# Hyperedge loop of a graph kernel: a fresh PSUM sum for every round, added on GpSimd, with the operand splits four tiles ahead

## The chip, the cores and the metric

The program runs on one core of a Trainium2 chip. The metric is the device time of one execution in microseconds (us). The core's engines run side by side and each takes its own instructions in order: TensorE (PE, with the loading of weights shown as PEld), VectorE (DVE), ScalarE (ACT), GpSimd (POOL), and SyncE for DMA. Semaphores order the work between engines.

## The reference, cut to what matters

Eight graphs (B) share 1024 nodes (N) and 64 hyperedges (E); features are 64 wide (F). The kernel computes four layers one after another, each with a residual and a layer norm. The change is in the first, in its hyperedge attention:

```
beta   = sigmoid((h @ a_gn)[:, None, :] + (agg @ a_ge)[:, :, None])
all_he = elu(beta * h + (1 - beta) * agg)            # for every (hyperedge, node) pair
coefs1 = softmax(where(H > 0, se, NEG), axis=-1)     # over the hyperedges of a node
g      = einsum('bne,benf->bnf', coefs1, all_he)
```

H is sparse (a node has about three hyperedges), so the kernel works only on the pairs that exist. What it sums for a node is the numerator (512 columns: 8 graphs times 64 features) and the denominator Z of the softmax (8 columns); g is their quotient.

## The kernel before

Nodes are on the 128 partitions, in NT = 8 tiles. The existing (node, hyperedge) pairs of a tile are listed one after another and taken in rounds of CHUNKS = 3 chunks (A, B, C) of 128 pairs. How many rounds a tile needs is known only on the chip (`first[t]` to `first[t + 1]`), so each engine runs, for each tile t, a loop `Fori(first[t], first[t + 1]) as j`. With this input every tile takes one round (line 908, which runs three times in a round, runs 24 times), so there are eight turns of the loop.

What one round does, by engine and line:

- DVE `from_first` and `to_last` (L742, L745) build NSF, the one-hot matrix that says which node each pair belongs to. They do it for the next round. `edges` (L749) builds EST, the same for hyperedges, from the sums that PE made (`edge_rows`, L655).
- PE `turn_edges` (L665) and `turn_nodes` (L660) transpose EST and NSF into PSUM bank 6. ACT copies them out as SELF and SELG (L828) and as NST (L866); `nodes_copy` (L831) makes NSG, a copy of NSF.
- PE `small_sums` (L671, L672) fetches the logits' parts, `gather` (L677 to L680) fetches h (as a high part HPH and a low part HPL) and agg for the pairs of a chunk. Chunk C is gathered in its own round, chunks B and A in the round before.
- DVE `mix` (L778), `shift` (L783), ACT `grow` (L862), DVE `bend` (L787) make the elu of a chunk; GpSimd multiplies it with the softmax weights CC (L908, and L903 for CC itself).
- PE `scatter` (L711) multiplies the result with NST and adds it to PSUM bank 4; the three matmuls of L733 add the weights to bank 7.

PSUM sums of a tile run over all its rounds. They are set to zero by a product of zeros at the head of each tile (L703, L704, bf16), and at the end of the tile ACT copies them out to GN and ZS (L886, L887). PE waits for that copy (`acc_out`) before it sets the banks to zero again. The order within each engine is written out by hand.

The high part HPH of h is made by ACT (L825) and the low part HPL by GpSimd (`low`, L895), each two tiles ahead: tiles 0 and 1 before the loop, tile t + 2 at the end of tile t. Also at the end of tile t, DVE takes the reciprocal of Z of tile t - 1 (L814) and GpSimd scales GN of tile t - 1 by it (L914); tile 7 is scaled by DVE after the loop (L816, L818). The block then ends, and the next block of the kernel begins on PE at L1026.

## Time and profile before

| | |
|---|---|
| median of 3 runs | 904.74 us (903.09, 904.74, 904.85) |
| the profiled execution | 903.21 us in all, its span 901.4 us |
| TensorE | 740.9 us busy, 82% of the span |
| VectorE | 439.6 us, 49% |
| ScalarE | 336.2 us, 37% |
| GpSimd | 293.2 us, 33% |
| mean granted clock of TensorE | 0.906 of full speed |
| the loop of this change on PE | from 152.4 us (first L703) to 241.7 us (end of the last L733) |

The span runs from the first to the last instruction; the device time of the same execution is 1.8 us longer. Busy times overlap, so they don't add up to the span. In the rows below, times are microseconds from the start of the span; "x3" is a count of instructions that the view has merged; a bracket behind a row tells how long the engine had been idle and which instruction (or "issue": nothing that the profile shows) ended that. A mean of one instruction is in nanoseconds.

### The profile page before, as it was taken

The numbers are of one execution on the slowest core, as the hardware profiler recorded it, in microseconds if no ns is written. First come the engines' busy times: TensorE is split into PE (matmuls) and PEld (weight loads), VectorE is DVE, ScalarE is ACT, GpSimd is POOL, SyncE is SP. The second block draws the span as 40 slices with busy tenths as digits, with TensorE's granted clock in tenths as the row PEclk, the third lists the DMA queues.
The fourth block names the chain that finished last, engine by engine and source line by source line (L and its number), as shares of the span: only waits on it lengthen the run. The fifth ranks groups of instructions, "written<-read, shape, count | busy, mean of one in ns | idle before, by whom it ended". The sixth has DMA issues, their size and how long they took to land. (4 is left out here: it accounts for less than half of the span.)

```text
span 901.4 us, 10005 instructions
## 1 busy us (share of the span) xinstructions
PE 740.9 (82%) x3518; PEld 506.5 (56%) x3518; DVE 439.6 (49%) x982; ACT 336.2 (37%) x628; POOL 293.2 (33%) x265
## 2 busy tenths in 40 slices
PE   3956985898897549899898983997888888899990
PEld 3646874666664448533232322786666666678880
DVE  1484353777448741245464666311355464562165
ACT  1741212445464121256353542222233536363110
POOL 0430001445365420000003149001356565651055
PEclk9967995999999669999998996899999899999995
DMA  8200002000000000000000000000000000000013
GB/s 278 80 14 1 1 1 93 1 1 1 1 1 1 0 1 1 1 0 1 1 0 1 0 12 38 1 1 1 0 1 1 1 1 0 1 1 1 1 24 70
DMA packets 12949, 14.36 MB, mean 16 GB/s; under 512 B 9680, under 2 KB 9680, under 8 KB 12896
## 3 DMA queue, kind: packets, MB, share of 16 engines
q1 hardware_dynamic: 11408, 11.61, 4.0%
q10 hardware_dynamic: 1488, 2.06, 0.8%
q8 instruction: 32, 0.52, 0.2%
q14 instruction: 21, 0.17, 0.1%
HBM read 11.57 MB, written 2.10 MB: 15 GB/s over the span
## 5 line engine op out<-in xcount | busy, mean ns | idle before, releaser
L1619 DVE SCALAR_TENSOR_TENSOR arena<-PS,WT,arena 128x256 f32<-128x256 f32 x160 | 77.4, 484 | 88.0 <-PE PS L1736 64.3
L1329 DVE TENSOR_REDUCE arena<-PS 128x1 f32<-128x1024 f32 x64 | 75.5, 1220 | 76.3 <-PE PS L1165 76.3
L1252 ACT ACTIVATE arena<-PS,arena 128x1024 f32<-128x1024 f32 x64 | 70.8, 1110 | 72.4 <-DVE arena L1329 72.4
L1165 PE MATMUL PS<-arena 64*128 64x512 f32 x256 | 77.4, 626 | 4.8 <-ACT arena L1252 2.5
L163 POOL TENSOR_TENSOR LN_Y<-LN_V,CN 128x16 f32<-128x16 f32 (+1 forms) x17 | 50.2, 2951 | 87.6 <-DVE LN_V L155 87.6
L1723 PE MATMUL PS<-WH,KH 128*128 128x512 f32 x128 | 55.4, 432 | 25.4 <-ACT XX L1537 20.7
L1549 ACT ACTIVATE SY<-PS,WT 128x256 f32<-128x256 f32 x96 | 38.5, 471 | 100.2 <-DVE arena L1619 100.2
L1272 POOL TENSOR_TENSOR arena<-arena 128x128 f32<-128x128 f32 x32 | 12.9, 403 | 188.0 <-DVE arena L1333 188.0
L1183 PE MATMUL PS<-arena 128*64 128x512 f32 x256 | 63.6, 620 | 1.2 <-POOL arena L1272 1.1
L1165 PEld LDWEIGHTS PS<-arena 64*128 64x128 f32 x256 | 28.5, 187 | 51.4 <-issue 32.0
L1723 PE MATMUL PS<-WH,KL 128*128 128x512 f32 x128 | 52.2, 408 | 0.0
L1723 PE MATMUL PS<-WL,KH 128*128 128x512 f32 x128 | 51.9, 405 | 0.0
L1723 PEld LDWEIGHTS PS<-WH,KH 128*128 128x128 f32 x128 | 24.9, 195 | 38.6 <-ACT XX L1537 23.8
L1183 PEld LDWEIGHTS PS<-arena 128*64 128x64 f32 x256 | 16.2, 140 | 46.5 <-issue 44.1
L1461 POOL TENSOR_TENSOR KL<-XX,KH 128x1024 fp32r<-128x1024 f32 x8 | 19.0, 2379 | 64.9 <-ACT KH L1539 64.9
L908 POOL TENSOR_TENSOR arena<-arena,CC 128x512 f32<-128x512 f32 x24 | 25.0, 1043 | 43.3 <-DVE arena L787 43.3
L895 POOL TENSOR_TENSOR HPL<-arena,HPH 128x512 fp32r<-128x512 f32 x8 | 10.2, 1277 | 81.0 <-ACT HPH L825 81.0
L140 DVE BATCH_NORM_STATS2 LN_ST<-arena 128x6 f32<-128x64 f32 x256 | 35.3, 211 | 2.1 <-POOL arena L1480 1.6
L283 POOL TENSOR_TENSOR ADJL<-arena,ADJH 128x1024 fp32r<-128x1024 f32 x8 | 19.7, 2486 | 43.4 <-ACT ADJH L295 43.4
L1765 PE MATMUL PS<-ADJH,NH 128*128 128x512 f32 x128 | 33.4, 394 | 0.5 <-ACT NH L1560 0.5
L1774 PE MATMUL PS<-ADJH,NL 128*128 128x512 f32 x128 | 32.8, 390 | 0.0
L1041 PE MATMUL PS<-arena,WT 128*128 128x512 f32 x64 | 32.0, 647 | 0.0
(265 smaller groups left out, 1631.4 us busy)
## 6 DMA issues: line engine op xcount, KB each, us to landing
arena<-in_adj_tr SPq DMA_DIRECT2D x8, 512.0 KB, 8.3
arena<-in_x_tr SPq DMA_DIRECT2D x4, 512.0 KB, 9.3
arena<-in_x_nat SPq DMA_DIRECT2D x1, 2048.0 KB, 8.4
...
```

The source lines that it names most:

```text
L140: ins = dve.bn_stats(LN_ST[:, i, :], source(i))
L163: pool.tensor_tensor(LN_Y[:, at:at + n], LN_V[:, at:at + n], CN[:, C_NEGH:C_NEGH + n], ALU.pow).then_inc(ln_rstd, 1)
L1041: pe.matmul(PS[:, 4 + v % HRING, :], wt(W_FC + (b % 2) * P, P), FT[:, (2 if w else 0) + q % 2, half * HALF:(half + 1) * HALF], start=True, ...
L1165: ins = pe.matmul(banks("S", 2 * i + par)[:, half, :], KT[q % 2][r, tile(m)], QT[q % 2][r, c], start=True, stop=True)
L1183: ins = pe.matmul(PS[r, 6 + half, :], AVN[:, i % RING, par, :], EF[2 * (i % RING) + par][:, c], start=(m == 0), stop=(m == NT - 1), skip_g ...
L1252: act.activation(EF[2 * (i % RING) + par], banks("S", 2 * i + par).rearrange("p a c -> p (a c)"), ACT.Exp, bias=NMX[:, i, par:par + 1], ac ...
L1329: dve.tensor_reduce(NMX[:, i, par:par + 1], banks("S", 2 * i + par), AX.XY, ALU.max, negate=True).then_inc(max_ready, 1)
L1549: act.activation(groups(SY[:, n % SYS, :]), PS[:, four_banks(t, j), d * F:(d + 1) * F], ACT.Copy, scale=WT[:, e:e + 1]).then_inc(sy_ready, 1)
L1619: dve.scalar_tensor_tensor(acc, PS[:, four_banks(t, j), d * F:(d + 1) * F], WT[:, e:e + 1], acc, ALU.mult, ALU.add).then_inc(acc_step, 1)
L1723: ins = pe.matmul(acc, x[:, t % 2, b, :], w[:, k, c], start=(first and n == 0), stop=(not first and n == 2), skip_group_check=True)
L1765: pe.matmul(acc[:, half, :], NH[:, m, tile(q)], ADJH[:, m, c], start=(m == 0), stop=False, skip_group_check=True)
L1774: ins = pe.matmul(acc[:, half, :], NL[:, m, tile(q)], ADJH[:, m, c], start=False, stop=(m == NT - 1), skip_group_check=True)
```

## The change

- **Sums.** The products of zeros and `zero16` are gone. The first `scatter` of every round starts bank 4 afresh (`start=(c == A_)`), and likewise the first of the three L733 matmuls bank 7. After every round ACT copies bank 4 to ROUND_SUM (in XX, a tensor that a later stage uses too and that is now allocated earlier) and the Z columns to ROUND_Z, and GpSimd adds them to ZS and GN, which it has set to zero once before the loop. `acc_raw` says that ACT has copied, `acc_out` that GpSimd has added.
- **Order on PE.** The waits for `acc_out` at the head of a tile go; `scatter(A_)` waits for `acc_raw`. `scatter(A_)` goes behind `small_sums`, `scatter(B_)` behind `gather(A_)` and `turn_nodes`. `turn_nodes` reads NSG in place of NSF.
- **Order on DVE.** `from_first` and `to_last` go to the head of the round, ahead of the mixes; `bend` of A goes behind `edges`, `bend` of C behind `logits`.
- **Order on ACT.** The copy of NST goes from the head of a round to its end, before the copies of the sums.
- **Ahead.** The high and low parts are made four tiles ahead: tiles 0 to 3 before the loop, tile t + 4 at the end of tile t. On GpSimd `low` now stands behind L914's scaling.

```diff
@@ -233,7 +233,6 @@
         DG = arena[:, 0:B * E].rearrange("p (b e) -> p b e", e=E)
         SEB = arena[:, B * E:2 * B * E].rearrange("p (b e) -> p b e", e=E)
         LGM = arena[:, 2 * B * E:4 * B * E].rearrange("p (a b e) -> p a b e", a=2, e=E)
-        zero16 = sb("zero16", [P, 512], BF16)
         ONR = sb("ONR", [P, 2], F32R)
         rest_max = sb("rest_max", [P, NT + 1])
         has_rest = sb("has_rest", [1, 1], I32)
@@ -274,7 +273,6 @@
                 pool.memset(SM[:, :], 0.0).then_inc(sl, 1)
                 pool.memset(AGBD[:, :, :], 0.0).then_inc(zero_set, 1)
                 pool.memset(HM[:, :, :], 0.0).then_inc(zero_set, 1)
-                pool.memset(zero16[:, :], 0.0).then_inc(zero_set, 1)
                 pool.wait_ge(sl, 1)
                 pool.memset(SM[0:64, 16:17], 1.0).then_inc(zero_set, 1)
                 for t in range(NT):
@@ -455,7 +453,7 @@
                 link(dve.tensor_tensor(AGM[:, :, :], AGM[:, :, :],
                                        wt(W_GE, F).unsqueeze(1).broadcast_to([P, BP, F]), ALU.mult))
                 link(dve.tensor_reduce(ae[:, :], AGM[:, :, :], AX.X, ALU.add))
-                dve.wait_ge(zero_set, 4)
+                dve.wait_ge(zero_set, 3)
                 for par in range(2):
                     r = slice(64 * par, 64 * par + 64)
                     dve.tensor_scalar(SM[r, par:B:2], ae[r, :], 0.5, None, ALU.mult)
@@ -613,8 +611,9 @@
         CC = sb("CC", [P, CHUNKS, B])
         ZS = sb("ZS", [P, NT, B])
         iota = CN[:, C_IOTA:C_IOTA + ROUND].rearrange("p (c n) -> p c n", n=P)
-        SMALL_AT, ZN_AT = CHUNKS * E, 0
+        SMALL_AT = CHUNKS * E
         A_, B_, C_ = range(CHUNKS)
+        AHEAD = 4
         bank_of = (0, 1, 0)
 
         fold_ready, agh_ready, agl_ready, agn_ready, hph_ready, hpl_ready = (
@@ -625,7 +624,10 @@
         ts_ready, lg_ready, thh_ready, xc_ready, be_ready, cc_ready, gath_ready, m_ready, z_ready, e_ready, t_ready, w_ready = (
             sem(s) for s in ("ts_ready", "lg_ready", "thh_ready", "xc_ready", "be_ready", "cc_ready", "gath_ready", "m_ready",
                              "z_ready", "e_ready", "t_ready", "w_ready"))
-        acc_done, acc_out, rn_ready, g_done = (sem(s) for s in ("acc_done", "acc_out", "rn_ready", "g_done"))
+        acc_done, acc_raw, acc_out, rn_ready, g_done = (sem(s) for s in ("acc_done", "acc_raw", "acc_out", "rn_ready", "g_done"))
+        XX = sb("XX", [P, B, 2, F])
+        ROUND_SUM = XX[:, 0:B // 2, :, :].rearrange("p b k f -> p (b k f)")
+        ROUND_Z = sb("ROUND_Z", [P, B])
 
         def first_rounds(eng):
             return [eng.value_load(first_i[0:1, t:t + 1], min_val=0, max_val=NT * ROUNDS) for t in range(NT + 1)]
@@ -657,7 +659,7 @@
 
                 def turn_nodes():
                     for c in range(CHUNKS):
-                        ins = pe.transpose(PS[:, 6, tile(c)], NSF[:, c, :], ident)
+                        ins = pe.transpose(PS[:, 6, tile(c)], bits(NSG[:, c, :]), ident)
                     ins.then_inc(nt_ready, 1)
 
                 def turn_edges():
@@ -698,17 +700,15 @@
                 pe.wait_ge(agl_ready, 1)
                 pe.nop().then_inc(acc_done, 1)
                 for t in range(NT):
-                    if t >= 1:
-                        pe.wait_ge(acc_out, t)
-                    pe.matmul(PS[:, 4, :], zero16[:, 0:P], zero16[:, :], start=True, stop=False, skip_group_check=True)
-                    pe.matmul(PS[:, 7, ZN_AT:ZN_AT + B], zero16[:, 0:P], zero16[:, 0:B], start=True, stop=False, skip_group_check=True)
                     pe.wait_ge(hpl_ready, min(t + 2, NT))
                     with pe.Fori(first[t], first[t + 1]) as j:
                         k_next, t_next = next_round(j, t, first)
 
                         def scatter(c):
                             pe.wait_ge(w_ready, CHUNKS * j + (c + 1))
-                            return pe.matmul(PS[:, 4, :], NST[:, c, :], S1[:, c, :], start=False, stop=True, skip_group_check=True)
+                            if c == A_:
+                                pe.wait_ge(acc_raw, j + 1)
+                            return pe.matmul(PS[:, 4, :], NST[:, c, :], S1[:, c, :], start=(c == A_), stop=(c == C_), skip_group_check=True)
 
                         pe.wait_ge(ns_ready, j + 2)
                         edge_rows(t_next)
@@ -717,20 +717,20 @@
                         pe.wait_ge(nst_out, j + 1)
                         pe.wait_ge(est_ready, j + 2)
                         turn_edges()
-                        scatter(A_)
                         pe.wait_ge(self_ready, j + 2)
                         small_sums(t_next)
+                        scatter(A_)
                         pe.wait_ge(nsg_ready, j + 2)
                         pe.wait_ge(selg_ready, j + 2)
                         pe.wait_ge(z_ready, CHUNKS * j + 2)
                         gather(t_next, B_)
-                        scatter(B_)
                         pe.wait_ge(z_ready, CHUNKS * j + 3)
                         gather(t_next, A_)
                         turn_nodes()
+                        scatter(B_)
                         scatter(C_)
                         for c in range(CHUNKS):
-                            ins = pe.matmul(PS[:, 7, ZN_AT:ZN_AT + B], NST[:, c, :], CC[:, c, :], start=False, stop=True,
+                            ins = pe.matmul(PS[:, 7, 0:B], NST[:, c, :], CC[:, c, :], start=(c == A_), stop=(c == C_),
                                             skip_group_check=True)
                         ins.then_inc(acc_done, 1)
 
@@ -786,33 +786,32 @@
                             dve.wait_ge(e_ready, CHUNKS * j + (c + 1))
                             dve.scalar_tensor_tensor(S1[:, c, :], S1[:, c, :], 1.0, S0[:, c, :], ALU.min, ALU.max).then_inc(t_ready, 1)
 
+                        dve.wait_ge(nsg_ready, j + 1)
+                        from_first(at).then_inc(ns_half, 1)
+                        dve.wait_ge(ns_half, j + 2)
+                        to_last(at).then_inc(ns_ready, 1)
                         dve.wait_ge(be_ready, j + 1)
                         mix(B_, 1)
                         mix(A_, 2)
-                        dve.wait_ge(selg_ready, j + 1)
-                        dve.wait_ge(nt_ready, j + 1)
-                        from_first(at).then_inc(ns_half, 1)
                         shift(A_, 2)
-                        dve.wait_ge(ns_half, j + 2)
-                        to_last(at).then_inc(ns_ready, 1)
                         shift(B_, 1)
-                        bend(A_)
                         dve.wait_ge(r_ready, j + 2)
                         dve.wait_ge(sT_ready, j + 1)
                         edges(k_next)
+                        bend(A_)
                         mix(C_, 3)
                         bend(B_)
                         shift(C_, 3)
                         dve.wait_ge(small_ready, j + 2)
                         dve.wait_ge(cc_ready, j + 1)
                         small_out()
-                        bend(C_)
                         dve.wait_ge(ts_ready, j + 2)
                         logits()
+                        bend(C_)
                     if t >= 1:
-                        dve.wait_ge(acc_out, t)
+                        dve.wait_ge(acc_out, first[t] + 1)
                         dve.reciprocal(ZS[:, t - 1, :], ZS[:, t - 1, :]).then_inc(rn_ready, 1)
-                dve.wait_ge(acc_out, NT)
+                dve.wait_ge(acc_out, first[NT] + 1)
                 dve.reciprocal(ZS[:, NT - 1, :], ZS[:, NT - 1, :]).then_inc(rn_ready, 1)
                 dve.wait_ge(rn_ready, NT)
                 dve.tensor_tensor(groups(GN[:, NT - 1, :]), groups(GN[:, NT - 1, :]), spread(ZS[:, NT - 1, :]), ALU.mult)
@@ -839,6 +838,7 @@
                 def likely():
                     act.activation(XC[:, :, :], LG[:, :, :], ACT.Exp).then_inc(xc_ready, 1)
 
+                act.nop().then_inc(acc_raw, 1)
                 act.wait_ge(fold_ready, 1)
                 act.activation(AGS[:, :], PS[:, 7, :], ACT.Copy).then_inc(agh_ready, 1)
                 high(0)
@@ -855,15 +855,16 @@
                 sigmoid()
                 act.wait_ge(lg_ready, 1)
                 likely()
+                act.wait_ge(nt_ready, 1)
+                edges_out(NST, nst_out)
+                for t in range(2, AHEAD):
+                    high(t)
                 for t in range(NT):
                     with act.Fori(first[t], first[t + 1]) as j:
                         def grow(c):
                             act.wait_ge(z_ready, CHUNKS * j + (c + 1))
                             act.activation(S1[:, c, :], S0[:, c, :], ACT.Exp, bias=CN[:, C_M1:C_M1 + 1]).then_inc(e_ready, 1)
 
-                        act.wait_ge(nt_ready, j + 1)
-                        act.wait_ge(acc_done, j + 1)
-                        act.activation(NST[:, :, :], PS[:, 6, 0:ROUND].rearrange("p (c n) -> p c n", n=P), ACT.Copy).then_inc(nst_out, 1)
                         grow(A_)
                         grow(B_)
                         act.wait_ge(sT_ready, j + 2)
@@ -880,11 +881,14 @@
                         act.wait_ge(lg_ready, j + 2)
                         act.wait_ge(cc_ready, j + 1)
                         likely()
-                    if t + 2 < NT:
-                        high(t + 2)
-                    act.wait_ge(acc_done, first[t + 1] + 1)
-                    act.activation(GN[:, t, :], PS[:, 4, :], ACT.Copy)
-                    act.activation(ZS[:, t, :], PS[:, 7, ZN_AT:ZN_AT + B], ACT.Copy).then_inc(acc_out, 1)
+                        act.wait_ge(nt_ready, j + 2)
+                        act.wait_ge(acc_done, j + 2)
+                        edges_out(NST, nst_out)
+                        act.wait_ge(acc_out, j + 1)
+                        act.activation(ROUND_SUM, PS[:, 4, :], ACT.Copy)
+                        act.activation(ROUND_Z[:, :], PS[:, 7, 0:B], ACT.Copy).then_inc(acc_raw, 1)
+                    if t + AHEAD < NT:
+                        high(t + AHEAD)
 
             @block.gpsimd
             def _(pool):
@@ -894,8 +898,11 @@
                     pool.wait_ge(hph_ready, t + 1)
                     pool.tensor_tensor(HPL[:, t, :], HP[:, t, :], bits(HPH[:, t, :]), ALU.subtract).then_inc(hpl_ready, 1)
 
-                low(0)
-                low(1)
+                for t in range(AHEAD):
+                    low(t)
+                pool.memset(ZS[:, :, :], 0.0)
+                pool.memset(GN[:, :, :], 0.0).then_inc(acc_out, 1)
+                pool.wait_ge(acc_out, 1)
                 for t in range(NT):
                     with pool.Fori(first[t], first[t + 1]) as j:
                         pool.wait_ge(xc_ready, j + 1)
@@ -907,12 +914,16 @@
                             pool.wait_ge(t_ready, CHUNKS * j + (c + 1))
                             pool.tensor_tensor(groups(S1[:, c, :]), groups(S1[:, c, :]), spread(CC[:, c, :]),
                                                ALU.mult).then_inc(w_ready, 1)
-                    if t + 2 < NT:
-                        low(t + 2)
+                        pool.wait_ge(acc_raw, j + 2)
+                        pool.wait_ge(acc_out, j + 1)
+                        pool.tensor_tensor(ZS[:, t, :], ZS[:, t, :], ROUND_Z[:, :], ALU.add)
+                        pool.tensor_tensor(GN[:, t, :], GN[:, t, :], ROUND_SUM, ALU.add).then_inc(acc_out, 1)
                     if t >= 1:
                         pool.wait_ge(rn_ready, t)
                         pool.tensor_tensor(groups(GN[:, t - 1, :]), groups(GN[:, t - 1, :]), spread(ZS[:, t - 1, :]),
                                            ALU.mult).then_inc(g_done, 1)
+                    if t + AHEAD < NT:
+                        low(t + AHEAD)
 
 
         FT = feature_major(0)
@@ -1356,7 +1367,6 @@
         X2 = node_major(3)
         XA = node_major(4)
         X3 = node_major(3)
-        XX = sb("XX", [P, B, 2, F])
         ZH = rounded("ZH", 5 * SLOT, [P, NT, BF])
         ZL = rounded("ZL", 6 * SLOT, [P, NT, BF])
         AH = rounded("AH", 0, [P, NT, BF])
```

## Rows read from the trace of the kernel before

**Rows 1.** Two turns: length; busy PE, PEld, DVE, ACT, POOL (instructions); TensorE clock, DMA.

```profile
177.90:188.60 10.70, 9.46 (x51) 6.71 (x51) 8.21 (x18) 5.49 (x14) 5.60 (x6) 1.00 0.01 2
188.60:200.50 11.90, 10.88 (x50) 7.57 (x51) 8.18 (x18) 5.50 (x14) 5.60 (x6) 0.86 0.00 0
```

**Rows 2.** Timeline from the end of one round's sums to the next: start, length, engine, line.

```profile
175.77 0.73 PE L733 MATMUL PS<-CC,arena 128*128 128x8 f32 x6
...
176.54 0.60 ACT L886 ACTIVATE arena<-PS 128x512 f32<-128x512 f32 x1 [2.85 <-PE PS L733]
...
177.26 0.10 PEld L703 LDWEIGHTS PS<-zero 128*128 128x128 bf16 x1 [0.84 <-ACT ZS L887]
...
177.46 1.39 ACT L862 ACTIVATE arena<-arena,CN 128x512 f32<-128x512 f32 x2
...
177.92 0.88 PE L655 MATMUL PS<-arena 128*128 x6 [0.26 <-issue]
...
178.97 0.87 DVE L749 TENSOR_SCALAR arena<-PS,CN 128x128 f32<-128x128 f32 x3
...
179.98 0.52 PE L665 MATMUL PS<-CN,arena 128*128 128x128 f32 x3 [0.20 <-DVE arena L749]
...
180.34 1.02 PE L711 MATMUL PS<-arena 128*128 128x512 f32 x2
...
180.42 0.68 DVE L787 SCALAR_TENSOR_TENSOR arena<-arena 128x512 f32<-128x512 f32 x1
180.54 0.49 ACT L828 ACTIVATE SELF<-PS 128x384 fp32r<-128x384 f32 x1 [1.69 <-PE PS L665]
...
181.20 0.29 PE L671 MATMUL PS<-SM,SELF 128*128 128x17 f32 x2
...
182.46 0.48 PE L677 MATMUL PS<-HPH,NSG 128*128 x1
...
184.53 1.28 POOL L895 TENSOR_TENSOR HPL<-arena,HPH 128x512 fp32r<-128x512 f32 x1
...
185.77 1.04 POOL L914 TENSOR_TENSOR arena<-arena,ZS 128x512 f32<-128x512 f32 x1
...
186.44 0.73 PE L733 MATMUL PS<-CC,arena 128*128 128x8 f32 x6
```

**Rows 3.** The page's costliest groups: GpSimd's multiplication by the weights.

```profile
L908 POOL TENSOR_TENSOR arena<-arena,CC 128x512 f32<-128x512 f32 x24 | 25.0, 1043 | 43.3 <-DVE arena L787 43.3
```

**Rows 4.** Groups of GpSimd's instructions by shape: count, busy us, mean ns, idle before.

```profile
L1480 POOL TENSOR_TENSOR arena<-arena,AGBD 128x512 f32<-128x512 f32 x4 | 5.2, 1292 | 0.6
L903 POOL TENSOR_TENSOR CC<-XC,TS 128x24 f32<-128x24 f32 x8 | 2.0, 246 | 6.8 <-PE PS L733 5.7 <-ACT XC L840 1.1
...
L275 POOL MEMSET AGBD<- 128x512 f32 x1 | 0.5, 524 | 0.0
L276 POOL MEMSET HM<- 128x136 f32 x1 | 0.2, 211 | 0.0
```

**Rows 5.** Timelines of DVE and GpSimd in the stage behind the loop.

```profile
265.37 1.23 DVE L952 TENSOR_TENSOR arena<-arena,KP 128x1024 f32<-128x1024 f32 x1
265.45 3.35 POOL L984 TENSOR_TENSOR arena<-arena 128x1024 f32<-128x1024 f32 x1
266.63 3.26 DVE L955 TENSOR_TENSOR arena<-arena 128x1024 f32<-128x1024 f32 x1
```

**Rows 6.** Timeline of the first round: turned nodes, first scatter, last sums.

```profile
152.70 0.49 ACT L866 ACTIVATE arena<-PS 128x384 f32<-128x384 f32 x1 [3.14 <-PE PS L660]
...
158.85 1.14 PE L711 MATMUL PS<-arena 128*128 128x512 f32 x2
...
165.06 0.73 PE L733 MATMUL PS<-CC,arena 128*128 128x8 f32 x6
```

**Rows 7.** Timeline of the loop's end and of the next block's first PE work.

```profile
240.96 0.73 PE L733 MATMUL PS<-CC,arena 128*128 128x8 f32 x6
...
242.66 0.69 DVE L818 TENSOR_TENSOR arena<-arena,ZS 128x512 f32<-128x512 f32 x1
...
243.66 1.24 PE L1026 MATMUL PS<-CN,arena 128*128 128x128 f32 x8 [1.98 <-PEq L642]
```

## The prediction, as it was put on record

> **What bounds the kernel now.** I read the page's head first (TensorE 82% busy, GpSimd 33%), then the busy time by stretch, then the timeline of one turn of the loop, since only there does an average turn into an order. In a turn PE is busy for 9.46 of 10.70 us; the next turn lasts 11.90 with nothing different in it but a granted clock of 0.86, that is, a piece of it at the lower of the two levels, 1.2 GHz [rows 1]. So PE bounds the loop, with one hole. The timeline shows the hole [rows 2]: the sums end at 176.50 (175.77 + 0.73; I call this moment Z), ACT copies bank 4 and Z out, PE is released at 177.26, sets the banks to zero, and begins the next round's products at 177.92, 1.42 after Z. From Z to Z (187.17) the turn takes 10.67. The page's groups show what GpSimd does meanwhile: its 24 multiplications of 1.04 us have 43.3 us of idle time before them, all ended by DVE [rows 3]. It is an engine with time to spare, and its end-of-tile work (`low` at 184.53, the scaling at 185.77, done at 186.81) lies ahead of Z, where nobody waits for it [rows 2]. That last point decides my forecast.
>
> **What the change takes away.** The two products of zeros and PE's wait for ACT: PE can begin `edge_rows` right behind Z, because `to_last` now stands at the head of DVE's round. The most this can give: from Z, edge_rows 0.88, edges 0.87, turn_edges 0.52, the SELF copy 0.49 [rows 2], with signals 3.0 us. (ACT gives the same: 1.15 for its copies, below, and 1.39 for two `grow`.) Then small_sums, 1.26 (181.20 to 182.46), then scatter A and the rest of the turn. The rest is 6.83 before (180.34 to 187.17), with the small sums in it, so 5.57 without them. 3.0 + 1.26 + 5.57 = 9.85, 0.8 less than 10.67. What had hidden the SELF copy was scatter A; it now stands behind small_sums, and this price is in the 3.0.
>
> **What it puts in the way.** Scatter A needs GpSimd's product w A. Before w A, GpSimd must now, in program order, wait for ACT's copy of the round's sums, add them, scale the tile before (L914), make `low(t + 4)`, and make CC. All of it was done before Z or didn't exist; now all of it begins after Z. Step by step, from Z:
> - ACT: NST copy, then the two copies. Before, the two took until 0.76 (177.26). With a copy of about 0.5 ahead, of which some 0.1 overlaps the next, `acc_raw` comes at 1.15.
> - GpSimd: the ZS add, 8 columns, isn't in the trace; CC with 24 columns takes 0.25 [rows 4], so 0.2. The GN add is two plain operands of 512 columns, as L1480, 1.29 [rows 4] (from below, the 1.04 of L914, whose second operand is a broadcast [rows 2]). Done at 2.65.
> - L914 1.04, `low` 1.24 by the distance to the next start (184.53 to 185.77) [rows 2], CC 0.2, w A 1.04 [rows 3] and a signal: 6.2.
> - PE's remaining 5.57: Z again at 11.8.
>
> So that is for tiles 2 to 4 (turns in which both L914 and `low` stand ahead). Turn 1 has no L914: 10.8. Turns 5 to 7 have no `low`: 10.55. This is by GpSimd's order alone.
>
> **The price of sharing.** GpSimd's work behind Z reads SBUF while DVE runs `bend` (L787, 0.68 [rows 2]), whose two inputs are both in SBUF. Before, bend and GpSimd hardly overlap. Elsewhere in this trace they do [rows 5]: L984 on GpSimd starts 0.08 after DVE's L952 and lasts 3.35; DVE's L955 starts at 266.63, and though it's of L952's shape (1.23) it takes 3.26, ending 1.09 after L984 (268.80). Each waited until the other was through; only about 0.14 of its time overlapped. So bend A, ready near 2.0, waits for the GN add, runs 0.54 past it, and L914 waits for bend A; bend B then goes between L914 and `low` in the same way. Each handover costs GpSimd 0.54 less 0.10 to 0.14, about 0.44; two make 0.9. Turns: 12.7 (three), 11.7 (turn 1), 11.45 (three). I take this case; the bound from below is no price at all.
>
> The Trainium skill has this as a rule: SBUF — State Buffer, section "Who interferes with whom", says that a DVE instruction with two SBUF inputs and a GpSimd instruction that reads SBUF take an exclusive lock, the later one blocking fully. By that rule the trace agrees, with the 3.26 against 1.23; the rule speaks against this change, and without it the sum below is 5.6 instead of 12.4.
> Of GpSimd's records the skill says (Perfetto Trace Analysis, section "Per-engine timelines") that one should go by the distance from start to start and not by the reported span. By that the multiplications would count a few hundredths less each, and the sum some 0.1 less a turn.
>
> **The sum.** Turns 1 to 7 took 241.69 - 165.79 = 75.9 [rows 6, 7]. After: 11.7 + 3 x 12.7 + 3 x 11.45 = 84.15, so +8.2. The 75.9 holds the slow-clock piece of one turn, 1.2 [rows 1]; whether it comes again is even, so +0.6.
>
> First turn: the turned nodes are out at 152.66 (L866 begins at 152.70). Then NST, `high(2)`, `high(3)` on ACT; `low(2)` can begin near 153.8, both end near 156.3. Then GN is set to zero: 4096 columns. 136 columns take 0.21 and 512 take 0.52 [rows 4], 0.83 ns each, so 3.5 (eight times 0.52, 4.2, from above; it can't be hidden since `acc_out` is waited for right behind). CC and w A end at 161.3. Scatter A starts then and not at 158.85 [rows 6], but the small sums are done by that time, and 5.57 later it is 166.9 against 165.79: +1.1.
>
> End: before, Z to the last multiplication's end was 1.66 (241.69 to 243.35), and the next block's PE began 0.3 later [rows 7]. After, acc_raw 1.15, adds to 2.65, reciprocal and multiplication: 3.6. But GpSimd scales tile 6 just then (2.65 to 3.7), with L818 also reading two SBUF inputs, so 4.2. +2.0 to +2.5; I take 2.5.
>
> 8.2 + 0.6 + 1.1 + 2.5 = +12.4. Removed besides: one zero16 fill at the start, under the input's loading, and nothing else; priced at nothing. Turning NSG in place of NSF costs the same, as the shape is the same. On the profiled execution (903.21, its span 901.4 and 1.8 around it) this gives 915.6; the median of the runs is 1.5 higher, 904.74, and gives 917.1. I say 917.
>
> **The rivals.**
> - *Only the queue, no lock* (the bends escape the overlap): turns 10.8, 3 x 11.8, 3 x 10.55 = 77.85, +1.95; with 0.6, 1.1 and 2.0 this is +5.6: 910.3. For it: bend A may slip in before the GN add starts. Against: rows 5. Chance 0.20.
> - *The hole closes and GpSimd keeps up*: PE's own 9.85 decides, seven turns give 7 x (10.84 - 9.85) = 6.9 against the mean turn of before, less 3.1 for first turn and end, about -3.5: 901. It needs w A by 4.3 after Z; the break-even is a turn of 10.4, w A by 4.8. GpSimd's shortest tail (no `low`) is 1.15 + 0.2 + 1.29 + 1.04 + 0.2 + 1.04 = 4.9, so its true times would have to be well under the records. For it: its spans are rough. Against: its back-to-back starts (184.53, 185.77) agree with them. Chance 0.06.
> - *No change*: the same with w A near 4.8: 904.7. Chance 0.04.
> - *The clock falls too*: PE now stands still for 2 to 3 us in every turn, ahead of scatter A. For it: the hole before, 1.42 us, went with one such fall in two turns shown [rows 1, 2], and PE's hole grows. Against: the other turn had the same hole and none. A turn's piece at the low level costs 1.2 [rows 1]; in four to seven turns, +5 to +8: 922 to 925. Chance 0.10.
> - The forecast, queue and lock: 0.60, its own range 914 to 920.
>
> **How the numbers follow.** About 0.2% (1.8 us) is what a measurement of this kernel can tell from no change. Slower by more: 0.60 + 0.20 + 0.10 = 0.90. Within: 0.04. Faster: 0.06. The range takes in the first two cases and the edge of the clock's: 908.5 to 921.
>
> **What the profile after would show.** Right: the first L711 of a round starts 6 to 7.3 us after Z, behind a wait for GpSimd's multiplication; GpSimd's GN add starts 1.2 to 1.4 after Z, and its L914, `low`, CC follow without a wait for another engine; turns of tiles 2 to 4 are 1.2 longer than those of 5 to 7; `bend` of A and B last over 1 us where a GpSimd record lies beside them. PE starts `edge_rows` within 0.2 of Z. Wrong: `bend` stays at 0.68 (the lock), L711 waits for nothing (the queue), PE's clock falls in most turns, or the zero fill takes far from 3.5 us.

## The result, and the profile after

The changed kernel takes 931.62 us (median of 4 runs, 928.07 to 933.20), the kernel before 903.91 on the same chip (902.92 to 904.85): a ratio of 1.0301 [1.0266, 1.0337]. It is slower, as forecast, but by 27.7 us where I had said 12.4, and outside the range.

The profiled execution took 930.43 us, its span 928.6; TensorE's mean granted clock is 0.896 (before 0.906). First the page's groups that wait for each other: the end of a row is the idle time ahead of the group and what ended it.

```profile
L711 PE MATMUL PS<-arena 128*128 128x512 f32 x48 | 29.9, 737 | 17.3 <-POOL arena L915 17.3
L899 POOL TENSOR_TENSOR HPL<-arena,HPH 128x512 fp32r<-128x512 f32 x8 | 12.4, 1560 | 86.3 <-ACT HPH L824 86.3
```

PE now waits 17.3 us for GpSimd ahead of its scatters (L711): 4.59 in the first round, 2.25 to 2.40 in turns 2 to 4, about 1.4 in the other four; before, it had no such wait. The busy time by stretch, cut at the moments Z (the ends of the rounds' L733 sums), answers to [rows 1]: length; busy PE, PEld, DVE, ACT, POOL; TensorE clock, DMA.

```profile
169.66:183.10 13.44, 10.93 (x49) 7.51 (x50) 10.04 (x17) 5.12 (x13) 7.01 (x7) 0.87 0.00 0
183.10:198.86 15.76, 12.26 (x51) 8.57 (x50) 10.38 (x17) 5.23 (x13) 8.35 (x8) 0.78 0.00 1
198.86:213.61 14.75, 11.41 (x49) 7.93 (x50) 10.39 (x17) 5.23 (x13) 8.35 (x8) 0.77 0.00 1
213.61:227.87 14.26, 10.77 (x51) 7.44 (x50) 10.39 (x17) 5.24 (x13) 8.35 (x8) 0.88 0.01 2
227.87:241.09 13.22, 10.95 (x51) 7.53 (x50) 10.32 (x17) 4.72 (x12) 6.78 (x7) 0.87 0.00 0
...
190.50:196.50 6.00, 6.00 (x14) 4.10 (x15) 3.94 (x6) 0.00 (x0) 2.34 (x2) 0.50 0.00 0
```

Two things are to be read there. PE is not only idle longer, its busy time grew too, from 9.46 [rows 1] to 10.8 to 12.3, for the same matmuls (less the two products of zeros). And no turn has the clock 1.00; the last row is a piece of the second turn at 0.50, the 1.2 GHz level, with PE busy all through. The timeline of that turn shows how it comes about (start, length, engine, line), for [rows 2]:

```profile
183.20 0.49 ACT L827 ACTIVATE arena<-PS 128x384 f32<-128x384 f32 x1 [6.82 <-PE PS L733]
...
184.33 0.21 POOL L919 TENSOR_TENSOR ZS<-ZS,ROUND_Z 128x8 f32<-128x8 f32 x1 [5.64 <-ACT ROUND_Z L889]
...
184.49 1.27 POOL L920 TENSOR_TENSOR arena<-arena,XX 128x512 f32<-128x512 f32 x1
...
185.41 0.90 DVE L787 SCALAR_TENSOR_TENSOR arena<-arena 128x512 f32<-128x512 f32 x1 [0.55 <-ACT arena L866]
185.72 1.49 POOL L923 TENSOR_TENSOR arena<-arena,ZS 128x512 f32<-128x512 f32 x1
...
186.42 0.40 PE L673 MATMUL PS<-SM,SELF 128*128 128x17 f32 x2 [0.90 <-ACT SELF L827]
...
187.18 1.71 POOL L899 TENSOR_TENSOR HPL<-arena,HPH 128x512 fp32r<-128x512 f32 x1
...
188.85 0.23 POOL L910 TENSOR_TENSOR CC<-XC,TS 128x24 f32<-128x24 f32 x1
...
189.24 3.60 POOL L915 TENSOR_TENSOR arena<-arena,CC 128x512 f32<-128x512 f32 x3 [0.17 <-POOL CC L910]
...
189.52 1.31 DVE L787 SCALAR_TENSOR_TENSOR arena<-arena 128x512 f32<-128x512 f32 x1
...
190.33 2.08 PE L711 MATMUL PS<-arena 128*128 128x512 f32 x2 [2.40 <-POOL arena L915]
...
198.13 0.73 PE L733 MATMUL PS<-CC,arena 128*128 128x8 f32 x6
```

From Z (183.10) GpSimd works without a pause: the ZS add, the GN add, the scaling (L923), `low` (L899), CC, w A (L915). Scatter A (L711) starts at 190.33, 7.23 after Z, and then takes 2.08 for what took 1.02 [rows 2]: PE had stood still for 2.40, and in that wait, at about 189.7, the granted clock went to the lower level, until about 196.6. In the other turns too it falls once, from 0.5 us before such a wait begins to 1.1 us after it has ended. The rest of the turn, from scatter A to the next Z, takes 8.53 and not 5.57. `bend` (L787) lasts 0.90, 0.93 and 1.31 for A, B and C beside GpSimd's records, 0.68 when alone [rows 2]. PE has a second hole that the kernel before had not, ahead of its small sums (L673), where it waits for the SELF copy: 0.90 in turns 1 to 4, 0.66 in turns 5 to 7.

All seven turns, each as (Z to scatter A) + (rest): 6.24 + 7.20, 7.23 + 8.53, 7.23 + 7.52, 7.23 + 7.03, 6.00 + 7.22, 6.00 + 7.18, 5.99 + 7.16; in all 97.76 against 75.90. GpSimd ahead of the first round, for [rows 6], and the loop's end, for [rows 7]:

```profile
153.70 3.04 POOL L899 TENSOR_TENSOR HPL<-arena,HPH 128x512 fp32r<-128x512 f32 x2 [5.25 <-ACT HPH L824]
156.69 0.15 POOL L903 MEMSET ZS<- 128x64 f32 x1
156.77 3.52 POOL L904 MEMSET arena<- 128x4096 f32 x1
160.94 0.23 POOL L910 TENSOR_TENSOR CC<-XC,TS 128x24 f32<-128x24 f32 x1 [0.66 <-POOL arena L904]
161.35 2.49 POOL L915 TENSOR_TENSOR arena<-arena,CC 128x512 f32<-128x512 f32 x2 [0.18 <-POOL CC L910]
...
268.65 0.20 POOL L919 TENSOR_TENSOR ZS<-ZS,ROUND_Z 128x8 f32<-128x8 f32 x1 [5.77 <-ACT ROUND_Z L889]
268.81 1.26 POOL L920 TENSOR_TENSOR arena<-arena,XX 128x512 f32<-128x512 f32 x1
270.03 1.04 POOL L923 TENSOR_TENSOR arena<-arena,ZS 128x512 f32<-128x512 f32 x1
...
270.34 1.28 DVE L817 TENSOR_TENSOR arena<-arena,ZS 128x512 f32<-128x512 f32 x1
271.93 1.30 PE L1037 MATMUL PS<-CN,arena 128*128 128x128 f32 x5 [4.50 <-PEq L644]
```

Scatter A of the first round starts at 162.44, Z comes at 169.66 (before 165.79): +3.9. The next block's PE begins 4.51 after the last Z (267.42), before 1.97: +2.5. So 21.9 + 3.9 + 2.5 = 28.3; the rest of the program is 1.1 shorter, and the spans differ by 27.2.

### The profile page after: what moved, and what is told of

It reads as the page before. It is cut to its first block and busy times, and to the rows that moved or that the text cites. A ratio compares the mean times of both kernels' runs of the same rounds, so it can differ in the third digit from the quotient of the medians.

```text
span 928.6 us, 9999 instructions
## 1 busy us (share of the span) xinstructions
PE 751.0 (81%) x3502; PEld 513.1 (55%) x3502; DVE 458.9 (49%) x982; ACT 334.6 (36%) x629; POOL 316.7 (34%) x282
## 5 line engine op out<-in xcount | busy, mean ns | idle before, releaser
L1283 POOL TENSOR_TENSOR arena<-arena 128x128 f32<-128x128 f32 x32 | 12.9, 403 | 186.9 <-DVE arena L1344 186.9
L711 PE MATMUL PS<-arena 128*128 128x512 f32 x48 | 29.9, 737 | 17.3 <-POOL arena L915 17.3
L899 POOL TENSOR_TENSOR HPL<-arena,HPH 128x512 fp32r<-128x512 f32 x8 | 12.4, 1560 | 86.3 <-ACT HPH L824 86.3
L1484 POOL TENSOR_TENSOR YP<-YP,SY 128x256 f32<-128x256 f32 x32 | 23.8, 743 | 22.3 <-ACT SY L1559 18.9
```

## The experiments

Times are medians beside runs of the kernel before on the same chip, whose medians are 902.74 us for 1 to 4, 900.84 for 5 to 8, 902.87 for 9 to 12 and 904.34 for 13 to 16. A ratio is to that kernel; it is taken over the runs and differs a little from the quotient of the medians. The turns are those of one profiled execution each. The part of the program behind the loop, which no edit touches, takes 655.7 to 662.6 us in these profiles, so a few us between two medians are no measure of the turns. "Products of zeros" compute nothing: they write a bank that is overwritten later.

**1. The fill of GN and ZS ahead of the first low parts.**

```diff
-                for t in range(AHEAD):
-                    low(t)
                 pool.memset(ZS[:, :, :], 0.0)
                 pool.memset(GN[:, :, :], 0.0).then_inc(acc_out, 1)
+                for t in range(AHEAD):
+                    low(t)
```

> The changed kernel with one edit: GpSimd sets GN and ZS to zero before it makes the first low parts, in time in which it had nothing to do, and not behind them. My theory: in the first round the 3.5 us fill stands between the low parts and the first product that PE waits for, so scatter A starts 4.2 us earlier (at about 158.2 us and not 162.4), PE hardly stands still, its clock stays up and the rest of the round takes 5.6 and not 7.2 us: 5 to 6 us less in all, near 926. All later turns as they were. Rival (the fill lies beside other work, and the first round waits for its small sums or its copies): less than 1 us.

926.69 us, 1.0259 [1.0222, 1.0296]: 23.9 us above the kernel before, not 27.7. Scatter A of the first round starts at 158.47, not 162.44, so the start that the first round lost was the fill's place. The other half of the theory missed: the clock falls in this round too (157.4 to 164.2), its rest takes 8.31 and not 5.6, and Z comes only 2.9 earlier. That 926 was met all the same is luck. The waits of the turns are as before this edit (6.24, three of 7.23, three of 6.00 to scatter A), their rests 1.5 longer in all.

**2. Scaling and `low` inside the round, ahead of its wait for the sums** (the same work where each tile has one round, as with these inputs).

```diff
+                        if t >= 1:
+                            pool.wait_ge(rn_ready, t)
+                            pool.tensor_tensor(groups(GN[:, t - 1, :]), groups(GN[:, t - 1, :]), spread(ZS[:, t - 1, :]),
+                                               ALU.mult).then_inc(g_done, 1)
+                        if t + AHEAD < NT:
+                            low(t + AHEAD)
                         pool.wait_ge(acc_raw, j + 2)
```

> The changed kernel with GpSimd's scaling of the tile before and its low part moved ahead of its wait for the round's sums (inside the round, which is the same where a tile has one round, as with this input). Theory, queue on GpSimd plus the clock: behind the end of the sums only the addition, CC and the first product are left, the product is there 4.3 us after it, when PE has just done its small sums, PE waits for nothing, its clock stays up: turns of 9.9 to 10.4 us in place of 13.2 to 15.8, in all 24 to 28 us less, 904 to 908, no worse than the kernel before by more than 4. Rival A, the new order on PE is what costs (the copy of the transposed edges lies open): turns stay above 12. Rival B, the clock falls for a reason other than PE's wait: the wait goes, turns of 11.5 us, about 916.

926.82 us, 1.0279 [1.0243, 1.0315]: the theory missed. Turns 1 to 4 stay above 12, as rival A had it, but for a reason that none of the three named. The timeline of turn 1, from Z = 168.02:

```profile
168.12 0.49 ACT L827 ACTIVATE arena<-PS 128x384 f32<-128x384 f32 x1 [7.93 <-PE PS L733]
...
169.04 0.64 ACT L824 ACTIVATE HPH<-arena 128x512 fp32r<-128x512 f32 x1
...
169.76 1.27 POOL L899 TENSOR_TENSOR HPL<-arena,HPH 128x512 fp32r<-128x512 f32 x1 [6.73 <-ACT HPH L824]
...
174.77 2.07 PE L711 MATMUL PS<-arena 128*128 128x512 f32 x2 [1.92 <-POOL arena L915]
```

`low(t + 4)` needs ACT's `high(t + 4)`, which ACT makes behind its copies of the sums. So `low` can't come ahead of Z here, and the adds now stand behind it. Turns 5 to 7 have no `low` and are free of it. Turns 5 and 6 show the second thing:

```profile
223.28:233.43 10.15, 9.29 (x49) 6.57 (x48) 8.40 (x14) 4.72 (x12) 6.32 (x7) 1.00 0.00 0
233.43:248.96 15.53, 13.87 (x51) 9.97 (x50) 10.97 (x21) 4.95 (x12) 6.25 (x7) 0.67 0.01 1
```

Both have no wait for GpSimd. The first is the turn the change could have had, 10.15; the second has the same work at clock 0.67 and takes 15.53 (turn 7: 11.66 at 0.85).

**3. Products of zeros in PE's wait**, the same kernel otherwise: nothing is taken from GpSimd, only PE's standing still.

```diff
                         small_sums(t_next)
+                        for _ in range(20 if t == 0 else 12 if 2 <= t <= 4 else 7):
+                            pe.matmul(PS[:, 7, 64:64 + 440], zero16[:, 0:P], zero16[:, 0:440], start=True, stop=True)
                         scatter(A_)
```

> The changed kernel with products of zeros (bf16, 440 columns, into columns of bank 7 that nobody reads) put on PE between its small sums and scatter A: 20 in the first round, 12 in rounds 2 to 4, 7 in the others, which fill most of its wait for GpSimd. They compute nothing. Theory, PE's standing still lets its clock fall: scatter A starts as late as before (7.2 and 6.0 us after the end of the sums), but the rest of the turn takes 5.6 in place of 7.0 to 8.5 us, in all 10 to 14 us less, 918 to 922. Rival, the clock falls for another reason (or the end of a turn is long for its new order of instructions): no change, 930 to 933.

922.26 us, 1.0199 [1.0168, 1.0229]; the profiled execution is the slowest of six, 930.22. Turns 1 and 6:

```profile
169.57:181.40 11.83, 10.63 (x58) 7.19 (x57) 9.71 (x17) 5.13 (x13) 7.01 (x7) 1.00 0.01 1
238.14:249.74 11.60, 10.63 (x58) 7.19 (x57) 10.00 (x17) 4.72 (x12) 6.79 (x7) 1.00 0.00 0
```

Scatter A starts 6.24 and 6.01 after Z, as without the fills, and the rest is 5.59 in both: these are the turns of my forecast (11.7 and 11.45), to 0.15. In turns 2 to 5 and 7 the clock still fell, in part ahead of the fills (in turn 2 at 185.9, the fills begin at 186.24); they then ran at the lower level, twelve in 3.89, and past the wait (scatter A at 8.57, 9.56, 8.30, 6.40, 7.00). In turns 4 and 5 it fell with the fills already running, when only the hole ahead of the small sums was left. So turns 1 and 6 show what the rest of a turn costs when the clock stays up, and speak for PE's standing still in the wait as the cause; five turns of seven don't decide it, and as a cure these fills are a poor one. More on the cause comes from 13 and 16.

**4. `low` ahead of the wait as in 2, and in its old place a fill (1,400 columns) of the same length**, which reads nothing. It changes no result, as tiles ahead are set to zero again.

```diff
+                        if t + AHEAD < NT:
+                            low(t + AHEAD)
                         pool.wait_ge(acc_raw, j + 2)
                         ...
                     if t + AHEAD < NT:
-                        low(t + AHEAD)
+                        pool.memset(GN[:, t + 1:t + 4, :].rearrange("p t c -> p (t c)")[:, 0:1400], 0.0)
```

> The changed kernel with the low part made ahead of GpSimd's wait, and in its old place a fill with zeros of 1400 columns (about the same 1.26 us, of tiles of GN that are still zero), which reads nothing. The queue on GpSimd is as long as it was; only the sharing between bend of chunk B and the low part is gone. Theory, lock: bend of B takes no longer than bend alone beside the fill, the fill starts right behind the scaling, and scatter A of turns 1 to 4 starts 0.4 to 0.5 us earlier (5.8 and 6.8 in place of 6.24 and 7.23 us after the end of the sums), 1.5 to 2 us in all. Rival, no lock, GpSimd just takes this long: 7.2 stays.

939.06 us, 1.0410 [1.0368, 1.0451]. Missed, for the reason found in 2: `low` waits for ACT, so both it and the fill are behind Z (scatter A at 7.50, then 8.95 three times). It says nothing of the lock; 7 and 8 ask that again.

**5. The change's orders alone:** the sums as before (banks set to zero, ACT copies them once a tile, no adds on GpSimd), all orders of PE, DVE and ACT as changed.

```diff
+                    if t >= 1:
+                        pe.wait_ge(acc_out, t)
+                    pe.matmul(PS[:, 4, :], zero16[:, 0:P], zero16[:, :], start=True, stop=False, skip_group_check=True)
                     ...
-                        pool.tensor_tensor(ZS[:, t, :], ZS[:, t, :], ROUND_Z[:, :], ALU.add)
-                        pool.tensor_tensor(GN[:, t, :], GN[:, t, :], ROUND_SUM, ALU.add).then_inc(acc_out, 1)
```

> The changed kernel's orders on PE, DVE and ACT, its splits four tiles ahead and the turned NSG, but the sums as before (a tile's sums stay in PSUM, products of zeros, ACT copies them straight to GN and ZS; no addition on GpSimd). Theory: the orders alone cost little; PE is released 1.2 us after the end of the sums, the chain of edge rows, edges, turned edges and their copy ends at 4.5, small sums and the rest of 5.6: turns of 11.4 against 10.7, about 5 us more than the kernel before, near 908. Rival A, the orders are the main loss of the change: over 918. Rival B, they are a gain on their own: under 902.

925.44 us, 1.0278 [1.0206, 1.0350]. My own theory missed: rival A holds. Without the adds and with no wait for GpSimd in the turns, the loss is nearly the same. Turns 1 and 3:

```profile
165.23:181.25 16.02, 13.96 (x50) 9.95 (x50) 9.84 (x18) 5.35 (x13) 5.71 (x6) 0.68 0.00 0
194.76:206.70 11.94, 9.69 (x51) 6.77 (x50) 8.42 (x16) 5.24 (x13) 5.71 (x6) 1.00 0.00 1
```

A turn at full clock takes 11.94 (6.38 + 5.56); three of the seven took about 16 with the clock low for two thirds of them.

**6. All low parts, and ACT's high parts, ahead of the loop** (with 1), so that no `low` stands behind Z.

```diff
-        AHEAD = 4
+        AHEAD = NT
```

> The changed kernel with all eight high and low parts made before the loop (ACT's and GpSimd's idle time there) and GN set to zero before them; nothing but the scaling stays behind the addition. Theory: turn 1 (no scaling) needs no wait on PE, 9.9 to 10.4 us; turns 2 to 7 are as turns 5 to 7 of the changed kernel, scatter A 6.0 us after the end of the sums, 13.2 us each; first round over at about 163.5 instead of 169.7: 912 to 920. Rival (the low parts' cost is hidden): no more than e1, 926.

920.67 us, 1.0202 [1.0160, 1.0244], just above what was expected. Turn 1 takes 4.56 + 5.59 = 10.15; turns 2 to 7 take 6.00 + (7.16 to 8.05). Here too the queue is as forecast (5.9), and the clock takes 1.6 to 2.5 on top.

**7 and 8. The lock by itself.** As 6, with one more GpSimd operation in the tail of tiles 1 to 3, where `low` stood: in 7 the subtraction that `low` is, into a spare buffer; in 8 a fill of the same length, which reads nothing.

```diff
+                    if t < 4:
+                        pool.tensor_tensor(SPARE, bits(HPL[:, t, :]), bits(HPH[:, t, :]), ALU.subtract)
```

```diff
+                    if t < 4:
+                        pool.memset(GN[:, t + 1:t + 4, :].rearrange("p t c -> p (t c)")[:, 0:1400], 0.0)
```

> As e7_all_ahead, with a subtraction of the low part's shape (its result is not used) put on GpSimd behind the scaling, at the end of tiles 0 to 3, where the changed kernel makes its low parts. It reads SBUF as they do, but waits for nothing. Theory: turn 1 has scatter A 6.2 and turns 2 to 4 have it 7.2 us after the end of the sums, as in the changed kernel; 919 to 926.

> As e9_read_in_tail, with a fill with zeros of 1400 columns (1.26 us) in place of the subtraction: as long, but reads nothing. Theory, lock: bend of chunk B doesn't wait beside it, and it doesn't wait for bend; scatter A comes 0.4 to 0.5 us earlier than in e9 in turns 1 to 4 (5.8 and 6.8 us after the end of the sums), 1.5 to 2.5 us in all. Rival, no lock and only the length of GpSimd's work: as e9 within 0.1 us a turn.

928.38 us, 1.0290 [1.0242, 1.0338] and 924.25 us, 1.0257 [1.0218, 1.0297]. GpSimd's records of one tail, of 7 and then of 8:

```profile
183.59 1.71 POOL L929 TENSOR_TENSOR XX<-HPL,HPH 128x512 f32<-128x512 f32 x1
185.27 0.22 POOL L913 TENSOR_TENSOR CC<-XC,TS 128x24 f32<-128x24 f32 x1
```

```profile
180.62 1.26 POOL L928 MEMSET arena<- 128x1400 f32 x1
181.85 0.23 POOL L912 TENSOR_TENSOR CC<-XC,TS 128x24 f32<-128x24 f32 x1
```

Scatter A of turns 2 to 4 starts at 7.23, 7.23, 7.24 in 7 and at 6.76 three times in 8. The operation that reads takes 1.71 with a `bend` between, the one that only writes 1.26: 0.46 to 0.48 a turn, where I had priced a handover at 0.44. The waits of the turns make 1.9 of the 4.1 us between the two medians, as expected; the rest of the 4.1 isn't theirs. Experiment 7 lies 2.4 above its range.

**9. The add one round late**, so that GpSimd adds the sums of round j - 1 while PE works on j, with all of 6.

```diff
-                        pool.wait_ge(acc_raw, j + 2)
+                        pool.wait_ge(acc_raw, j + 1)
                         pool.wait_ge(acc_out, j + 1)
-                        pool.tensor_tensor(GN[:, t, :], GN[:, t, :], ROUND_SUM, ALU.add).then_inc(acc_out, 1)
+                        pool.tensor_tensor(g_sum, g_sum, ROUND_SUM.unsqueeze(1), ALU.add).then_inc(acc_out, 1)
```

> As e7_all_ahead, with the addition of a round's sums one round later: GpSimd adds the sums of round j - 1 behind the three products of round j, and those of the last round behind the loop. Behind the end of the sums only CC and the products are left. Theory, GpSimd's queue: no turn waits for it, each is like turn 1 of e7, 10.15 us where the clock stays up, the first round as in e7; with no fall of the clock about 897, 5 less than the kernel before; the hole of 0.7 to 0.9 us ahead of the small sums is left in every turn, so some falls of 1.6 to 5 us each must be expected: 896 to 906. Rival, the clock falls in most turns all the same: 908 to 915.

926.94 us, 1.0269 [1.0232, 1.0306]. Missed. There is no wait for GpSimd's w A any more and turns of 10.01 to 10.68 appear, but every second one takes 16.2 to 16.8, with the clock at 0.50 for 10.2 us:

```profile
179.20:189.40 10.20, 8.86 (x26) 6.54 (x26) 5.72 (x12) 3.90 (x9) 4.29 (x5) 0.50 0.01 2
```

Behind it stand new holes that I hadn't seen: DVE's reciprocal now waits for the late add, ahead of `from_first`, and PE's `edge_rows` comes 1.35 late.

**10. Experiment 9 with three products of zeros ahead of the small sums.** The edit is that of 13 below, with three.

> As e8_all_ahead_lag, with three products of zeros (bf16, 440 columns, into bank 1 before it is gathered into) on PE between the turned edges and the small sums, where PE waits for the copy of the turned edges. They compute nothing. Theory, PE's standing still is what lets the clock fall: the turns of e8 at the lower clock become turns at the full one, 10.15 to 10.4 us each, 895 to 900. Rival, the hole has nothing to do with it: as e8.

920.47 us, 1.0226 [1.0165, 1.0286]; turns 10.68, 13.23, 12.85, 16.42, 10.01, 17.13, 10.03: with this one hole filled the others still bring falls.

**11 and 12. The orders taken apart.** In 11 PE's order is that of before and the others (DVE's, ACT's, GpSimd's) are changed; 12 is the kernel before with PE's order alone:

```diff
                         turn_edges()
-                        scatter(A_)
                         pe.wait_ge(self_ready, j + 2)
                         small_sums(t_next)
+                        scatter(A_)
                         ...
                         gather(t_next, B_)
-                        scatter(B_)
                         pe.wait_ge(z_ready, CHUNKS * j + 3)
                         gather(t_next, A_)
+                        scatter(B_)
```

> As e5_orders_only, but with PE's order of before (scatter A ahead of the small sums, scatter B ahead of gather A): what is left of the change are DVE's and ACT's orders, the turned NSG and the splits four tiles ahead. Theory, after e5 (925.4): what e5 lost came from PE standing still twice in a turn, for ACT's copies (now 0.4 later) and for the copy of the turned edges; without the second, turns of about 11.1 us at full clock and falls in few of them: 904 to 912. Rival, the 0.4 us on ACT are enough for the clock: over 918.

> The kernel before with nothing but PE's order of after: scatter A behind the small sums, scatter B behind gather A and the turned nodes. Theory, after e5: the copy of the turned edges (0.5 us) lies open, small sums start 4.6 us after the end of the sums, scatter A 5.85, turns of 11.4 us at full clock, and the two holes together bring the clock down in several of the seven turns: 908 to 920. Rival A, the order alone is harmless: 901 to 906. Rival B, it is the whole loss of e5: 922 or more.

11: 929.43 us, 1.0297 [1.0262, 1.0331], missed; PE waits 1.11 for w A in the five turns at full clock, since DVE makes `edges` ahead of `bend` A and w A waits for that `bend` (its record starts 1.16 late for it); two turns take 16.0 and 16.1. 12: 918.08 us, 1.0200 [1.0139, 1.0261]. Its turns 1 to 3, and PE's holes in turn 2:

```profile
164.24:179.89 15.65, 13.88 (x49) 9.77 (x50) 7.97 (x18) 5.38 (x13) 5.59 (x6) 0.67 0.00 0
179.89:191.31 11.42, 9.47 (x50) 6.77 (x50) 7.93 (x17) 5.41 (x13) 5.60 (x6) 1.00 0.01 2
191.31:204.32 13.01, 11.05 (x49) 7.77 (x50) 8.14 (x19) 5.40 (x13) 5.59 (x6) 0.87 0.00 0
```

```profile
180.88 0.17 PE L704 MATMUL PS<-zero 128*128 128x8 bf16 x1 [0.98 <-ACT ZS L887]
...
184.38 0.40 PE L671 MATMUL PS<-SM,SELF 128*128 128x17 f32 x2 [0.58 <-ACT SELF L828]
```

PE's order costs 0.75 a turn at full clock (11.42 against 10.67), as scatter A no longer hides the SELF copy, and with this second hole of 0.58 the clock falls in four of seven turns: 1.6 where the low piece is short (13.01 - 11.42; 3.4 us at 0.5), 4.2 where it is long (15.65 - 11.42; 10.2 us).

**13. Experiment 12 with four products of zeros in that hole.**

```diff
                         turn_edges()
+                        pe.wait_ge(z_ready, CHUNKS * j + 2)
+                        for _ in range(4):
+                            pe.matmul(PS[:, 1, 0:440], zero16[:, 0:P], zero16[:, 0:440], start=True, stop=True)
```

> As e13_pe_order_only (918.1), with four such products of zeros between the turned edges and the small sums, where that kernel has its second hole, 0.6 us. The hole at the end of a turn stays. Theory: with one hole only, the clock does as in the kernel before, a low stretch in one or two turns of 3.4 us and none of 10; turns of 11.4 to 11.6 us otherwise: 906 to 912. Rival, the second hole doesn't matter to the clock: 916 to 920.

914.89 us, 1.0102 [1.0063, 1.0141]. Slower than expected, but no 10 us piece is left: three of 3.4 us, in turns of 12.5; the other four take 11.4 to 11.5. The profiled executions of 12 and 13 took 915.21 and 915.74: the seven turns are 8.1 us shorter in 13, but its first round ends 3.7 later and the part behind the loop is 5.0 longer.

**14. The kernel before with both its holes filled**, three products in the wait for ACT at the head of a tile and two ahead of the small sums (twelve in the first round).

```diff
+                    pe.wait_ge(m_ready, CHUNKS * first[t] + 1)
+                    for _ in range(3):
+                        pe.matmul(PS[:, 1, 0:440], zero16[:, 0:P], zero16[:, 0:440], start=True, stop=True)
                     pe.matmul(PS[:, 4, :], zero16[:, 0:P], zero16[:, :], start=True, stop=False, skip_group_check=True)
```

> The kernel before with products of zeros (bf16, 440 columns, into bank 1, which nobody reads at that time) on PE in its hole at the end of a tile: 3 ahead of its wait for ACT's copies, 2 (in the first round 12) behind the zeroing. They compute nothing. Theory, the lower clock follows PE's standing still: the low stretch of the first round (155.5 to 159) and the one of turn 3 (189.8 to 193.2) go, the turns stay 10.7 us: 898 to 901.5, against about 903. Rival, these stretches come from something else: 902 to 905.

899.89 us against 904.34, 0.9940 [0.9896, 0.9985]: the one version whose interval lies below the kernel before. Two of its turns; all seven take 10.54 to 10.82, none has a low piece:

```profile
177.15:187.97 10.82, 10.18 (x56) 6.94 (x55) 8.19 (x18) 5.46 (x13) 5.61 (x6) 1.00 0.01 2
187.97:198.69 10.72, 10.11 (x56) 6.94 (x55) 8.20 (x18) 5.46 (x13) 5.60 (x6) 1.00 0.00 0
```

Where the 4.4 us come from, the profile doesn't show. It is of the slowest of five executions (905.68; the fastest took 894.97): its seven turns take 74.84 us, 1.05 less than before, the first Z comes 0.7 later and the part behind the loop is 2.9 longer. That the fills take the loop's low pieces away is seen; that this is worth 4.4 us is not.

**15 and 16. The change with its waits removed:** as 9, with the reciprocal one tile later still and the fills of zeros made long before the loop; 16 adds four products of zeros a turn, as in 13.

```diff
-                    if t >= 1:
-                        dve.wait_ge(acc_out, first[t] + 2)
-                        dve.reciprocal(ZS[:, t - 1, :], ZS[:, t - 1, :]).then_inc(rn_ready, 1)
+                    if t >= 2:
+                        dve.wait_ge(acc_out, first[t - 1] + 2)
+                        dve.reciprocal(ZS[:, t - 2, :], ZS[:, t - 2, :]).then_inc(rn_ready, 1)
```

> As e8_all_ahead_lag, with what its trace showed amiss put right: the reciprocal on DVE (and the scaling on GpSimd) is that of two tiles before, so DVE doesn't wait for the late addition ahead of the next round's NSF; and GN is set to zero in the block before the loop, since its fill on GpSimd held DVE's first NSF for 3.2 us. Theory: PE begins a round at once after the sums, turns of 9.9 to 10.1 us at full clock; the small sums' hole of 0.7 us stays; one low stretch or none, 896 to 901, better than the kernel before. Rival, the small sums' hole alone brings the clock down in every second or third turn, 1.6 to 5 us each: 903 to 912.

> As e16_late_recip, with four products of zeros in the hole ahead of the small sums. Theory: no hole is left in a turn beyond 0.3 us, the clock stays up in all, turns of 10.0 to 10.3 us, 896 to 900. Rival: as e16.

15: 910.03 us, 1.0068 [1.0042, 1.0094]. Four turns take 10.00 to 10.03, close to PE's own 9.85 of the prediction, one 10.81, and two hold a low piece of 6.8 us and take 14.03 and 14.05. 16: 904.55 us, 0.9995 [0.9972, 1.0018]; every turn at full clock. Turn 3, whose length turns 1 to 6 share, and turn 7:

```profile
186.85:197.53 10.68, 10.02 (x54) 7.02 (x54) 9.91 (x18) 4.78 (x12) 6.18 (x8) 1.00 0.00 1
229.59:239.61 10.02, 9.80 (x52) 6.85 (x52) 6.47 (x14) 4.72 (x12) 5.83 (x8) 1.00 0.00 0
```

The 0.66 between them isn't the price of the fills, which turn 7 has too; DVE is what sets 10.68. `edges` (L759 here) of the two turns:

```profile
188.42 0.86 DVE L759 TENSOR_SCALAR arena<-PS,CN 128x128 f32<-128x128 f32 x3
...
230.49 0.87 DVE L759 TENSOR_SCALAR arena<-PS,CN 128x128 f32<-128x128 f32 x3 [0.58 <-PE PS L664]
```

In turn 7 it starts 0.90 after Z, as soon as PE's sums are there; in the other it starts at 1.57, straight behind DVE's own work. Ahead of that turn `from_first` and `to_last` took 1.04 and 1.55 beside GpSimd's third product and its late add, against 0.37 and 1.16 ahead of turn 7. Turn 6 of 15 shows the same without fills: it follows a turn at full clock, `edges` starts at 1.70, and it takes 10.81. Turns 1, 3 and 5 of 15, of 10.00, each follow a round with a low piece, in which DVE had got ahead of PE. And the end still costs 3.92 and not 1.98. No version with the change's scheme that was run beats the kernel before.

## Why the prediction was wrong

- **The queue behind Z, right.** Forecast from Z to scatter A: 6.1 in turn 1 (11.7 less 5.57), 7.1 in turns 2 to 4, 5.9 in turns 5 to 7; measured 6.24, 7.23, 6.00. With PE's rest at 5.57 the seven turns would have made 45.92 + 39.0 = 84.9 us; I had 84.15. The adds started at 1.23 and the GN add took 1.27, near the 1.15 and 1.29 worked out.
- **The lock, right.** Experiments 7 and 8 part it from the queue: 0.47 a turn for one handover. The Trainium skill says of this pair (SBUF — State Buffer, section "Who interferes with whom") that a DVE instruction with two SBUF inputs contends with a GpSimd instruction that reads SBUF and not with one that only writes; 1.71 against 1.26 agrees. The sign that `bend` of A and B would last over 1 us came only in part: A 0.90 in turns 2 to 4 and 1.42 in 5 to 7, B 0.92 to 0.93 in all six.
- **PE's rest of 5.57, wrong: the step that failed.** I carried it over from the turn at full clock. It was 7.03 to 8.53 in every turn, 51.84 in all against 39.0, so +12.9, since in each turn 3.4 or 6.8 us were at 1.2 GHz. The forecast missed the profiled execution by 14.8 (27.2 against 12.4): 12.9 here, 0.8 in the queue, 2.8 in the first round, less the 0.6 that I had put in for a low piece and the 1.1 won elsewhere. I had this as a rival, "the clock falls too", with 0.10, and priced it at 1.2 a turn for four to seven turns. The count came out, seven of seven; the chance and the price were off. The evidence that I used against it, one fall for two turns with the same hole, was of a hole that stayed as it was; my forecast put a second hole of 1.6 to 2.85 us into each turn (11.45 to 12.7 less PE's own 9.85), and the rival should have gone with it as its consequence, not beside it. And the price, read off the one short piece that the trace had, is that of short pieces only: 1.0 (5) to 1.6 for 3.4 us, 3.0 in turn 2 of the change for 6.8 us, 4.1 (5, 12) to 5.4 (2) for 10.2 us.
- **The cause.** That the longer rest is the lower clock is seen in every turn. That the clock falls because PE stands still is shown by the fills, which compute nothing: in 3 the same waits with PE kept busy give a rest of 5.59 at clock 1.00 in two turns of seven (none in the change); 16 has no fall where 15 has two of 6.8 us, 14 none where the kernel before has one, 13 three of 3.4 us where 12 has two such and two of 10.2. Which of PE's holes brings a given fall isn't shown.
- **The queue was not the only sufficient cause.** Experiment 5 says that without the adds on GpSimd the orders alone cost 24.6 us, and 12 that PE's order alone costs 15.2 (the seven turns by themselves: 22.1 and 15.6 more than before). I had costed the SELF copy that this order lays bare in PE's time, and not what one more hole does to the clock. The two causes don't add, as each by itself is enough to bring the clock down.
- **First round, +3.9 against +1.1.** The fill took 3.52 as forecast (3.5); CC came 0.66 behind it, the two low parts took 3.04 and not 2.5, and the low clock made the rest 7.22, 1.65 more. **End, +2.5 against +2.5.**
- **The "queue only" and "keeps up" rivals** are both out: `bend` did overlap and GpSimd did not keep up. The second had a gap besides: it took PE's own 9.85 as the turn, and 16 shows that with PE at full clock DVE makes it 10.68, what it was before.

Open: which hole brings the clock down and which doesn't. The kernel before has one of 1.42 a turn (PE idle for 1.02 of it) and fell once in seven; with 0.58 more (12) it fell in four of seven, two of them long. With that second hole filled (13) it still fell in three, and 11, with holes of 1.43 and 1.11 a turn, fell in two. A fall seems to prolong itself, as the holes inside a low piece remain, but no run tells this apart from chance. Why 5 has three long pieces and 12 two wasn't tried, nor why the first round and the part behind the loop differ by several us between profiles.
